# Transformer block on eight cores: the scalar engine's one-element copy after each softmax exponential is left out

## The chip, the cores and the metric

The program runs on all eight cores of one Trainium2 chip. Each core takes one of the eight sequences of the batch (4096 tokens of width 1024) and does the whole block on it; nothing passes between cores. The metric is the device time of the slowest core, in microseconds (us).

## What is computed

The reference adds to x (8 x 4096 x 1024) a full softmax attention of 16 heads over 4096 tokens, and after that a two-layer local-attention network. The change lies in the first part alone:

```
x = x + attn(layernorm(x));  x = x + ffn(layernorm(x))
q = einsum('bnd,hde->bhne', query, Wq) * scale     # E = 64, H = 16, scale = 1/8
k = einsum('bmd,hde->bhme', query, Wk);  v = einsum('bmd,hde->bhme', query, Wv)
attn = softmax(einsum('bhne,bhme->bhnm', q, k), axis=-1)
out = einsum('bhnm,bhme->bnhe', attn, v)
```

Then come two layers with a shifted token, a window of 512, xpos rotary tables, and a gated network of width 2730.

## The kernel before, in words

The instruction streams of the engines are written out by hand in program order. `op` (whose line 150 is the line of nearly every instruction in the profile) puts one instruction into an engine's list, with waits on semaphores ahead of it and increments behind it. For DVE and ACT, `op` adds two things on its own: a wait until every earlier instruction of the same engine has raised that engine's semaphore (`V` or `S`), and an increment by one when the instruction is done. `val('S')` is the count that the semaphore S will have after everything put into ACT's list so far. `sfence` puts a copy of one float (`fsc`, 1x1) into ACT's list and returns the count after it; `vfence` does the same on DVE.

Stage A (the first 5440 us or so) is the full attention. The 16 heads are taken in 4 groups of four (`grp`). A group first makes K (transposed, `KTg`) and V (`Vg`, 64 columns and one column of ones for each head) for all 4096 keys. Then, for each of 8 blocks of 512 queries (`qb`), it makes Q (`Qg`), runs for each of two head pairs (`p`) the inner loop over 32 chunks of 128 keys (`mc`), and multiplies the result by the output weights (`Wpg`). So the inner loop is run 4 x 8 x 2 = 64 times, with 32 chunks each.

One chunk of the inner loop is:

- S: two matmuls, one for each head of the pair, on two halves of the array (64 rows each), scores of 128 keys by 512 queries, into PSUM `pb1` for even and `pb3` for odd chunks. The first waits until the exponential of chunk mc-2 has read that PSUM tile.
- exp: one ACTIVATE on ACT, 128x1024, from `pb1` or `pb3` into `Pa` (even) or `Pb` (odd). It waits for S of its chunk and, through `op`, for every ACT instruction before it.
- the fence: a COPY of `fsc` on ACT. Its count is stored as `sexp[mc]`.
- AV: two matmuls (128 keys, 65 rows of output, 512 queries) from `Pa` or `Pb` that add to `pb5` and `pb6`. They wait for `sexp`.

TensorE's list holds S of chunk mc ahead of AV of chunk mc-1: S0, S1, AV0, S2, AV1, S3 and so on to AV31. Two waits tie the engines together: AV of chunk j waits for `sexp[j]`, and S of chunk j+2, which stands behind that AV, waits for the same count. In the text below a "pitch" is the time from the start of one exponential to the start of the next.

After the 32 chunks DVE takes the reciprocal of each head's sum (`drow`), TensorE spreads it, DVE scales into `Ost`, and the next pair's S may begin. In the profile all PSUM tiles (`pb0` to `pb7`) have the name `pb`.

The second part works in the same manner with buffers named `L0...` and `L1...` for its two layers. Its exponentials (`L0Ph`) have no copy behind each one: there the score matmuls wait for an ACTIVATE itself.

Of the kernel before, what the change touches and what calls it, by code (L numbers as in the profile page):

```python
# [97 lines left out]
class MK:  # L98
# [265 lines left out]
    def _stage_a(self):  # L364
# [127 lines left out]
        for grp in range(ngrp):  # L492
# [71 lines left out]
            for qb in range(NQB):  # L564
# [12 lines left out]
                for p in range(2):  # L577
                    sexp = {}
                    tavm = {}
                    p0exp = self.val('S')  # L580
                    for mc in range(33):
                        if mc < 32:
                            Sp = pb1 if mc % 2 == 0 else pb3
                            Pj = Pa if mc % 2 == 0 else Pb
                            wS = [('S', sexp[mc - 2])] if mc >= 2 else [('S', p0exp)]
                            self.op('T', 'matmul', Sp[:, 0:512],
                                    KT[p][0:64, mc * 128:(mc + 1) * 128],
                                    Qg[0:64, p * 512:(p + 1) * 512],
                                    start=True, stop=True, tile_position=(0, 0),
                                    wait=wS)  # L590
                            self.op('T', 'matmul', Sp[:, 512:1024],
                                    KT[p][64:128, mc * 128:(mc + 1) * 128],
                                    Qg[64:128, p * 512:(p + 1) * 512],
                                    start=True, stop=True, tile_position=(64, 0),
                                    inc=('T', 1))
                            ts = self.val('T')
                            we = [('T', ts)]
                            if mc - 2 in tavm:
                                we.append(('T', tavm[mc - 2]))
                            self.op('S', 'activation', Pj[:, :], Sp[:, :], AF.Exp,  # L600
                                    scale=0.125, wait=we)
                            sexp[mc] = self.sfence()
                        if mc >= 1:
                            j = mc - 1
                            Pj = Pa if j % 2 == 0 else Pb
                            self.wait('T', 'S', sexp[j])
                            self.op('T', 'matmul', pOa[0:65, :],
                                    Vg4[:, j, 2 * p, :], Pj[:, 0:512],
                                    start=(j == 0), stop=(j == 31))
                            self.op('T', 'matmul', pOb[0:65, :],  # L610
                                    Vg4[:, j, 2 * p + 1, :], Pj[:, 512:1024],
                                    start=(j == 0), stop=(j == 31),
                                    inc=('T', 1))
                            tavm[j] = self.val('T')
                    tav = self.val('T')
                    for hh, pO in ((0, pOa), (1, pOb)):
                        self.op('V', 'reciprocal', drow[0:1, :], pO[64:65, :],
                                wait=[('T', tav)] if hh == 0 else None, inc=('V', 1))
                        vr1 = self.vfence()
                        self.op('T', 'matmul', pm[0:64, 0:512], self.ones1b[0:1, 0:64],  # L620
                                drow[0:1, :], start=True, stop=True,
                                wait=[('V', vr1)], inc=('T', 1))
                        tb1 = self.val('T')
                        self.op('V', 'tensor_copy', dn[:, :], pm[0:64, 0:512], wait=[('T', tb1)])
                        self.op('V', 'tensor_tensor',
                                Ost[hh * 64:(hh + 1) * 64, p * 512:(p + 1) * 512],
                                pO[0:64, :], dn[:, :], op=ALU.mult, inc=('V', 1))
                    self.wait('T', 'V', self.vfence())
# [820 lines left out]
```

How the kernel before makes its waits and increments, by code:

```python
        def fn(e):  # L147
            for sm, v in wait:
                e.wait_ge(semh[sm], v)
            instr = getattr(e, meth)(*a, **kw)
            for sm, k in incv:
                instr.then_inc(semh[sm], k)
# [2 lines left out]
    def wait(self, eng, sem, v):  # L155
        semh = self.semh
        self.emit(eng, lambda e: e.wait_ge(semh[sem], v))
# [12 lines left out]
        def fn(e):  # L170
            for sm, v in toks:
                e.wait_ge(semh[sm], v)
```

## Time and profile before

| | us |
|---|---|
| median of two timed runs | 12493.09 (12472.9 and 12513.29) |
| the profiled execution, its time | 12375.73 |
| its span, first to last instruction of the slowest core | 12374.1 |
| ACT busy | 3587.4 (29% of the span) |
| TensorE matmuls busy | 6101.7 (49%) |
| DVE busy | 4237.4 (34%) |

The profile is of one execution, of its slowest core (core 0) where nothing else is said. Busy times are sums over the span, and the span holds stages with different limits, so a share says little by itself. PE is TensorE, PEld its weight loads. The granted clock is given in parts of full speed: 1.00 is 2.4 GHz, 0.50 is 1.2 GHz. In a timeline the columns are start (us from the span's start), duration (us), engine, line, operation, output<-input, shapes and count; neighbouring instructions of one kind are merged into one row with their count, and brackets hold the idle time of the engine before it and what ended it.

### The profile page before, as it was taken

How to read it: one execution, taken by the hardware profiler on the slowest of the kernel's cores; microseconds unless marked ns; L12 is line 12 of the kernel's file. 1: busy time of each engine (PE TensorE's matmuls, PEld its weight loads, DVE VectorE, ACT ScalarE, POOL GpSimd, SP SyncE). 2: the span in 40 equal slices, each digit the busy share in tenths (PEclk: the TensorE clock that was granted, in tenths of full speed). 3: DMA queues.
4: the chain of work that ended last, by engine and by line, in shares of the span. 5: the costliest groups of instructions: out<-in, count | busy, mean ns of one | idle time of the engine just before them, and what ended most of it. 6: DMA issues, size and time to landing. Idle time of an engine off the chain costs nothing.

```text
span 12374.1 us, 129139 instructions; the slowest of 8 cores (12332.9 to 12374.1 us)
## 1 busy us (share of the span) xinstructions
PE 6101.7 (49%) x36694; PEld 3084.5 (25%) x36694; DVE 4237.4 (34%) x8932; ACT 3587.4 (29%) x6788; POOL 270.1 (2%) x406
## 2 busy tenths in 40 slices
PE   2555555546555545533333333777733333346766
PEld 1111111112111211111111112665611111135665
DVE  5111221112111222235555553333345445523333
ACT  0555355544555245521111110111101111101111
POOL 0000000000000000000000000000000000000000
PEclk9788787778887777765555555888855555568888
DMA  3000001010000110120000003000010010041110
GB/s 116 14 14 14 21 12 17 14 18 14 14 14 14 35 40 28 35 62 17 17 23 29 17 18 75 22 28 28 19 44 17 17 34 17 18 86 42 33 41 28
DMA packets 237209, 361.42 MB, mean 29 GB/s; under 512 B 27664, under 2 KB 122512, under 8 KB 234468
## 3 DMA queue, kind: packets, MB, share of 16 engines
q0 software_dynamic: 51968, 101.01, 4.9%
q1 hardware_dynamic: 120036, 168.23, 4.3%
q10 hardware_dynamic: 64512, 83.91, 1.9%
q8 instruction: 315, 5.16, 0.2%
q14 instruction: 378, 3.10, 0.1%
HBM read 269.23 MB, written 134.35 MB: 33 GB/s over the span
## 4 chain that ended last, share of the span: by engine, by line
PE 33%; DVE 25%; ACT 22%; issue 9%; DMA 8%; DVEq 1%; ACTq 1%; POOL 0%; SPq 0%; POOLq 0%
PE pb L150 33%; ACT Pa L150 8%; ACT Pb L150 8%; DVE drow L150 3%; ACT fsc L150 3%; DVE fsc L150 2%; DVE L1drl L150 2%; DVE L0drl L150 2%; DMA yacc<-ysb 2%; DVE L0tmp L150 1%; ACT L0Ph L150 1%; DVE pb L150 1%; ACT L1Ph L150 1%; DVEq L149 1%; DMA L1dw<-w 1%
## 5 line engine op out<-in xcount | busy, mean ns | idle before, releaser
L150 ACT ACTIVATE Pa<-pb 128x1024 bf16<-128x1024 f32 x1024 | 1047.7, 1023 | 2558.2 <-PE pb L150 2473.1
L150 DVE RECIPROCAL drow<-pb 1x512 bf16<-1x512 f32 x128 | 429.0, 3352 | 3032.6 <-PE pb L150 3026.0
L150 ACT ACTIVATE Pb<-pb 128x1024 bf16<-128x1024 f32 x1024 | 1047.7, 1023 | 115.6 <-PE pb L150 22.4
L150 PE MATMUL pb<-Pa,Vg 128*65 128x512 bf16 x2048 | 655.5, 403 | 514.6 <-ACT fsc L150 508.5
L150 PE MATMUL pb<-Qg,KTg 64*128 64x512 bf16 x4096 | 842.3, 413 | 113.3 <-DVE fsc L150 113.3
L150 PE MATMUL pb<-Pb,Vg 128*65 128x512 bf16 x2048 | 653.6, 402 | 467.4 <-ACT fsc L150 465.0
L150 PE MATMUL pb<-L0dh,L0dw 128*128 128x256 bf16 x5632 | 703.1, 281 | 170.9 <-DVE fsc L150 170.9
L150 PE MATMUL pb<-L1dh,L1dw 128*128 128x256 bf16 x5632 | 702.3, 281 | 170.9 <-DVE fsc L150 170.9
L150 PEld LDWEIGHTS pb<-L0dh,L0dw 128*128 128x128 bf16 x5632 | 565.4, 101 | 261.1 <-issue 181.5
L150 PEld LDWEIGHTS pb<-L1dh,L1dw 128*128 128x128 bf16 x5632 | 565.4, 101 | 260.2 <-issue 181.5
L150 ACT COPY fsc<-fsc 1x1 f32<-1x1 f32 x2904 | 552.4, 190 | 255.3 <-ACT L1dgel L150 1.1
L150 DVE COPY fsc<-fsc 1x1 f32<-1x1 f32 x3161 | 448.2, 142 | 334.5 <-DVE pb L150 2.5
L150 PEld LDWEIGHTS pb<-Qg,KTg 64*128 64x128 bf16 x4096 | 202.1, 93 | 1017.5 <-issue 1017.1
L150 PE MATMUL pb<-Ost,Wpg 128*128 128x512 bf16 x512 | 259.1, 609 | 348.3 <-DVE fsc L150 348.3
L150 ACT ACTIVATE L1Ph<-pb,L1rk 128x512 bf16<-128x512 f32 (+1 forms) x480 | 253.0, 527 | 591.8 <-DVE fsc L150 563.5
L150 ACT ACTIVATE L0Ph<-pb,L0rk 128x512 bf16<-128x512 f32 (+1 forms) x480 | 253.0, 527 | 589.9 <-DVE fsc L150 522.8
L150 DVE TENSOR_TENSOR pb<-pb,M_sb 128x128 f32<-128x128 f32 x960 | 287.9, 300 | 340.0 <-PE pb L150 280.4
L150 PE MATMUL pb<-drow,ones1b 1*64 1x512 bf16 x128 | 76.9, 601 | 603.2 <-DVE fsc L150 603.2
L150 PE MATMUL pb<-L1du,L1dw 128*128 128x256 bf16 (+1 forms) x2816 | 364.9, 272 | 18.2 <-DVE fsc L150 18.0
L150 PE MATMUL pb<-L0du,L0dw 128*128 128x256 bf16 (+1 forms) x2816 | 365.0, 272 | 17.2 <-DVE fsc L150 17.2
L150 PEld LDWEIGHTS pb<-Pa,Vg 128*65 128x65 bf16 x2048 | 149.0, 112 | 823.4 <-issue 823.4
L150 PEld LDWEIGHTS pb<-Pb,Vg 128*65 128x65 bf16 x2048 | 148.5, 111 | 772.5 <-issue 772.5
(263 smaller groups left out, 7176.4 us busy)
## 6 DMA issues: line engine op xcount, KB each, us to landing
yacc<-ysb POOLq DMA_DIRECT2D x192, 256.0 KB, 4.1
xspan<-xT SPq DMA_DIRECT2D x16, 2048.0 KB, 10.2
yac<-yacc SPq DMA_DIRECT2D x64, 256.0 KB, 3.5
xsp<-xT SPq DMA_DIRECT2D x64, 256.0 KB, 3.9
R<-x1f ACTq DMA_DIRECT2D x64, 256.0 KB, 3.7
RA<-L0za ACTq DMA_DIRECT2D x64, 256.0 KB, 2.9
RZ<-L0dzot ACTq DMA_DIRECT2D x128, 128.0 KB, 1.7
RA<-L1za ACTq DMA_DIRECT2D x64, 256.0 KB, 3.0
```

Source lines behind the costliest of these rows:

```text
L149: e.wait_ge(semh[sm], v)
L150: instr = getattr(e, meth)(*a, **kw)
```

## The change

One expression in the inner loop of `_stage_a`: the count that is stored for chunk mc is that of the ACTIVATE itself, and the COPY behind it is no longer put into ACT's list.

```diff
                             self.op('S', 'activation', Pj[:, :], Sp[:, :], AF.Exp,
                                     scale=0.125, wait=we)
-                            sexp[mc] = self.sfence()
+                            sexp[mc] = self.val('S')
```

ACT's list from the first inner loop on, before (`fsc` is the copy; `pb1` and `pb3` are the two score tiles):

```order
3 L150 COPY fsc<-fsc 1x1 [waits S] x2
4 L150 ACTIVATE Pa<-pb1 128x1024 [waits T,S]
5 L150 COPY fsc<-fsc 1x1 [waits S]
6 L150 ACTIVATE Pb<-pb3 128x1024 [waits T,S]
7 L150 COPY fsc<-fsc 1x1 [waits S]
8 L150 ACTIVATE Pa<-pb1 128x1024 [waits T,S]
9 L150 COPY fsc<-fsc 1x1 [waits S]
```

ACT's list at the same place with the change:

```order
3 L150 COPY fsc<-fsc 1x1 [waits S] x2
4 L150 ACTIVATE Pa<-pb1 128x1024 [waits T,S]
5 L150 ACTIVATE Pb<-pb3 128x1024 [waits T,S]
6 L150 ACTIVATE Pa<-pb1 128x1024 [waits T,S]
7 L150 ACTIVATE Pb<-pb3 128x1024 [waits T,S]
8 L150 ACTIVATE Pa<-pb1 128x1024 [waits T,S]
```

One COPY goes for each exponential; each ACTIVATE keeps its wait for ACT's own count, which is now that of the ACTIVATE before it. TensorE's list is the same in both kernels, with the same waits. Here it is from the first chunk of the first loop on (`pb5` and `pb6` take the output of the two heads); `waits S` there is the count that now comes from the ACTIVATE:

```order
933 L150 MATMUL pb3<-Qg,KTg0 128x512 [waits S]
934 L150 MATMUL pb3<-Qg,KTg0 128x512
935 L150 MATMUL pb5<-Pa,Vg 65x512 [waits S]
936 L150 MATMUL pb6<-Pa,Vg 65x512
937 L150 MATMUL pb1<-Qg,KTg0 128x512 [waits S]
938 L150 MATMUL pb1<-Qg,KTg0 128x512
939 L150 MATMUL pb5<-Pb,Vg 65x512 [waits S]
940 L150 MATMUL pb6<-Pb,Vg 65x512
```

Nothing moved on TensorE, DVE, GpSimd or SyncE.

## Rows read from the trace of the kernel before

**Rows 1.** The cores: span and mean granted clock of the slowest

```profile
core 0: 12374.1 us, clock 0.729
```

**Rows 2.** The chain that ended last, by engine and by line

```profile
PE 33%; DVE 25%; ACT 22%; issue 9%; DMA 8%; DVEq 1%; ACTq 1%; POOL 0%; SPq 0%; POOLq 0%
PE pb L150 33%; ACT Pa L150 8%; ACT Pb L150 8%; DVE drow L150 3%; ACT fsc L150 3%; DVE fsc L150 2%; DVE L1drl L150 2%; DVE L0drl L150 2%; DMA yacc<-ysb 2%; DVE L0tmp L150 1%; ACT L0Ph L150 1%; DVE pb L150 1%; ACT L1Ph L150 1%; DVEq L149 1%; DMA L1dw<-w 1%
```

**Rows 3.** The page's costliest groups: busy us, mean ns | idle before, releaser

```profile
L150 ACT ACTIVATE Pa<-pb 128x1024 bf16<-128x1024 f32 x1024 | 1047.7, 1023 | 2558.2 <-PE pb L150 2473.1
...
L150 ACT ACTIVATE Pb<-pb 128x1024 bf16<-128x1024 f32 x1024 | 1047.7, 1023 | 115.6 <-PE pb L150 22.4
...
L150 ACT COPY fsc<-fsc 1x1 f32<-1x1 f32 x2904 | 552.4, 190 | 255.3 <-ACT L1dgel L150 1.1
```

**Rows 4.** Timeline, middle of an inner loop, 769 to 774 us

```profile
770.18 0.19 ACT L150 COPY fsc<-fsc 1x1 f32<-1x1 f32 x1
770.46 1.02 ACT L150 ACTIVATE Pa<-pb 128x1024 bf16<-128x1024 f32 x1
...
770.51 0.59 PE L150 MATMUL pb<-Pb,Vg 128*65 128x512 bf16 x2 [0.48 <-ACT fsc L150]
...
771.04 0.39 PE L150 MATMUL pb<-Qg,KTg 64*128 64x512 bf16 x2
771.57 0.19 ACT L150 COPY fsc<-fsc 1x1 f32<-1x1 f32 x1
771.85 1.02 ACT L150 ACTIVATE Pb<-pb 128x1024 bf16<-128x1024 f32 x1
```

**Rows 5.** Windows of 5 us between and inside inner loops: PEclk before the DMA share

```profile
950.00:955.00 5.00, 0.60 (x1) 0.12 (x1) 3.87 (x4) 0.00 (x0) 0.00 (x0) 0.50 0.00 0
...
965.00:970.00 5.00, 3.22 (x14) 0.85 (x14) 0.00 (x0) 4.36 (x8) 0.00 (x0) 1.00 0.00 0
```

**Rows 6.** Timeline, start of the inner loop at 957 us, and its end

```profile
957.55 1.02 ACT L150 ACTIVATE Pa<-pb 128x1024 bf16<-128x1024 f32 x1 [14.69 <-PE pb L150]
...
959.00 1.03 PE L150 MATMUL pb<-Pa,Vg 128*65 128x512 bf16 x2 [1.17 <-ACT fsc L150]
959.96 0.61 PE L150 MATMUL pb<-Qg,KTg 64*128 64x512 bf16 x2
...
960.50 1.06 PE L150 MATMUL pb<-Pb,Vg 128*65 128x512 bf16 x2
960.78 1.02 ACT L150 ACTIVATE Pa<-pb 128x1024 bf16<-128x1024 f32 x1 [0.54 <-PE pb L150]
...
963.91 1.02 ACT L150 ACTIVATE Pa<-pb 128x1024 bf16<-128x1024 f32 x1 [0.29 <-PE pb L150]
...
1001.68 1.02 ACT L150 ACTIVATE Pb<-pb 128x1024 bf16<-128x1024 f32 x1
...
1003.13 0.59 PE L150 MATMUL pb<-Pb,Vg 128*65 128x512 bf16 x2 [0.80 <-ACT fsc L150]
```

**Rows 7.** Timeline, window attention of layer 0, 6427 to 6430 us

```profile
6427.40 0.69 ACT L150 ACTIVATE L0Ph<-pb,L0rk 128x512 bf16<-128x512 f32 x1
...
6428.23 0.50 PE L150 MATMUL pb<-L0qf,L0kf 64*128 64x384 bf16 x2 [0.95 <-ACT L0Ph L150]
...
6428.56 1.47 ACT L150 ACTIVATE L0Ph<-pb,L0rk 128x512 bf16<-128x512 f32 x2 [0.47 <-DVE fsc L150]
```

**Rows 8.** Timeline, gated network of layer 0, 8620 to 8628 us, clock 1.00

```profile
8620.12 1.91 PE L150 MATMUL pb<-L0dh,L0dw 128*128 128x256 bf16 x16
...
8622.19 0.47 ACT L150 ACTIVATE L0dgel<-pb,L0b1t 128x256 f32<-128x256 f32 x1 [1.87 <-PE pb L150]
```

**Rows 9.** Timeline, first inner loop, 336 us, in a stretch of granted clock 0.81

```profile
336.20 0.69 PE L150 MATMUL pb<-Pa,Vg 128*65 128x512 bf16 x2 [0.33 <-ACT fsc L150]
...
336.83 0.44 PE L150 MATMUL pb<-Qg,KTg 64*128 64x512 bf16 x2
```

**Rows 10.** Window 2790 to 2850 us, core 2, making K and V

```profile
2790.00:2850.00 60.00, 55.13 (x372) 36.59 (x377) 31.70 (x97) 0.55 (x1) 0.00 (x0) 1.00 0.00 1
```

## The prediction

> **What bounds the kernel now.** I read the cores first, to see whose time counts: core 0 ends last, its span of 12374.1 us is the time to shorten [rows 1]. Then the chain that ended last. It has no single owner, but exponentials of the full attention (`Pa`, `Pb`) hold 16% of it and the one-element copy `fsc` on ACT another 3% [rows 2]. That is the copy that the change takes out, so it stands on the path somewhere. The groups say how much there is: 2 x 1024 exponentials of 1023 ns, and 2904 copies of 190 ns, of which 2048 go [rows 3]; the 64 inner loops have 32 chunks each, and 64 x 32 = 2048.
>
> Where the copy costs its time only the timeline shows. In the middle of a loop the exponential of 770.46 us ends at 771.48, the copy starts at 771.57, ends at 771.76, and the next exponential starts at 771.85 [rows 4]. So ACT works without a break: pitch 1.02 + 0.09 + 0.19 + 0.09 = 1.39 us, and the two starts lie 1.39 apart. TensorE waits for ACT: its AV pair starts 0.14 after the copy's end (770.37 to 770.51), with the copy as releaser. In this stretch ACT is the bound and everything else has slack.
>
> That holds for most pitches, not for all. Between loops TensorE is nearly idle and its granted clock is 0.50; inside it is 1.00 [rows 5]. The loop that begins at 957.55 starts at the low level: the AV pair takes 1.03 us in place of 0.59, the exponential of 960.78 is released by TensorE and not by ACT, and the fifth exponential (963.91) comes 6.36 us after the first, against 5.56 for four pitches of 1.39 [rows 6]. From there to the last one (1001.68) are 27 pitches in 37.77 us, 1.40 each. This loop takes 44.13 us from its first to its last exponential; in the timeline the other 63 look alike, with 3 to 5 long pitches at their start.
>
> **The change, part by part.** Removed: the copy (0.19) and one of the two gaps (0.09), 0.28 us for each exponential. Nothing is added and nothing is moved on another engine; TensorE's and DVE's instructions keep their order. What must be worked out is which limit comes next.
>
> ACT's own limit becomes 1.02 + 0.09 = 1.11 us. That two ACTIVATEs in a row have the same gap is seen in the second part: one of 128x512 takes 0.69, two take 1.47 together, so the gap is 0.09 [rows 7].
>
> The other limit is a round trip. The exponential of chunk j+2 needs S of chunk j+2, which stands behind AV of chunk j, which needs the exponential of chunk j. One trip covers two pitches. Its pieces:
> - the exponential, 1.023;
> - its end to the start of AV, without the copy. The nearest row is a score matmul that waits for an ACTIVATE directly: 6427.40 + 0.69 = 6428.09, start 6428.23, so 0.14 [rows 7]. It is the same 0.14 as behind the copy, so no extra price for leaving the fence;
> - start of AV to start of S, 770.51 to 771.04, 0.53, and S itself, 0.39 [rows 4];
> - end of S to start of exp. In the loop at low clock: 959.96 + 0.61 = 960.57, start 960.78, 0.21 [rows 6]. In the gated network at clock 1.00: 8620.12 + 1.91 = 8622.03, start 8622.19, 0.16 [rows 8].
>
> With 0.21 the trip is 1.023 + 0.14 + 0.53 + 0.39 + 0.21 = 2.293, or 1.147 a pitch; with 0.16 it is 1.122. With the copy it was 2.573, or 1.287, hidden below 1.39. So the cover of the round trip is gone: it is just above ACT's 1.11, and what is late next is S. I take 0.21, since that row is the same pair of instructions at the same place. A pitch in the fast stretch then gains 1.393 - 1.147 = 0.246. The bounds are 0.28 (ACT alone sets it) and, from the clock (below), 0.173.
>
> At the low clock TensorE itself is near its own limit: AV to S 0.96, S to AV 0.54, 1.50 a pitch [rows 6]. The second and third exponentials come 0.28 earlier (957.55 + 1.11; and 960.50, the trip from the first being 0.28 shorter). The fourth and fifth follow at 1.50 to 1.54, so the fifth comes at about 963.58 in place of 963.91: 0.33 gained, where 4 x 0.28 would be 1.12. That the clock rises at the same moment is assumed; TensorE is as busy there as before.
>
> At the end of the loop the last AV waits for the last exponential: 1001.68 + 1.02 = 1002.70, start 1003.13 [rows 6]. It gains the 0.28 whole, since DVE's reciprocal stands right behind it.
>
> Sum for a loop: 0.33 + 27 x 0.246 + 0.28 = 7.25 us. Times 64: 464 us, call it 465. All of it is on the path, since in the loop DVE, SyncE and GpSimd have nothing that others wait for; what follows (reciprocals, projection, the write of `yacc` by DMA) is released by the loop's end and only shifts. The loads of the next group's weights stand behind those writes in GpSimd's queue and shift with them, so they hide no more and no less. The second part of the program is untouched.
>
> Against its own time the profiled execution would go from 12375.7 to about 11911. The two timed runs lie 0.8 to 1.1% above it (median 12493.1), and I have no row that says why; I subtract the same 465 from the median: 12028 us. The level stays an unknown of some 117 us.
>
> **The rivals.**
>
> A. ACT alone sets the pitch, because S reaches exp in 0.16 or less and two trips interleave. For it: the 0.16 of rows 8 and a difference of only 0.034 between the two limits. Against it: the loop's own 0.21. Per loop 0.33 + 27 x 0.28 + 0.28 = 8.17, times 64 = 523: 11970.
>
> B. The clock goes down to the middle level under the denser work. TensorE's S and AV take 0.98 us of each pitch: 70% of 1.39 before, 86% of 1.147 after. In its first loop core 0 was granted 0.81, with AV to S 0.63 and S 0.44 [rows 9]: the trip is 1.023 + 0.14 + 1.07 + 0.21 = 2.44, 1.22 a pitch, gain 0.173. Before, that was hidden below 1.39, so the loop did not show it. Per loop 0.33 + 27 x 0.173 + 0.28 = 5.28, times 64 = 338: 12155. Against it: with TensorE busy for 55.13 of 60 us in making K and V, more than the 86%, core 2 was granted 1.00 [rows 10].
> The Trainium skill, "TensorE: Matmul & The Clock Gate", Part 1 (the clock gate), says that a peak-current limiter takes a die to 13/16 of the clock once three of its cores run dense matmuls. That speaks for B in every loop, as all cores do the same thing at nearly the same time. Rows 10 do not bear it out: the other cores of that die were in the same stage in that window. By that rule the sum would be that of B.
>
> C. The time goes up: TensorE does not leave its low clock in the loops, or leaves it late. The place is the fourth and fifth pitch of each loop, where it now rises. Then the pitch is TensorE's 1.50 against 1.39: 27 x 0.107 = 2.89 lost a loop, less 0.61 gained at both ends, 2.28 x 64 = 146 us, 12639. It decides the sign once fewer than 7 of the 27 later pitches are at full clock (0.246 f + 0.61 = 0.107 (27 - f)). Against it: denser work was granted 1.00, and I see no row where more work lowered it to 0.50.
>
> D. The copy was not what AV waited for, and AV still starts 0.42 after the exponential. Then ACT is free but the trip stays at 2.573: pitch 1.287, gain 27 x 0.106 = 2.86 + 0.3 a loop, some 200 us, 12290. Against it: the direct wait of rows 7.
>
> **How the numbers follow.** My forecast 0.74, A 0.12, B 0.09, C 0.02, D 0.03. The forecast's own doubt is small in the mechanism (between 1.12 and 1.16 a pitch, 40 us or so) and larger in the level of the runs (117 us). The range reaches down to A measured at the level of the profiled execution (12376 - 523 = 11853, of which I leave the last bit out) and up to B from the median (12155): 11870 to 12155. A measurement of this kernel can tell about 2% from no change, that is 250 us. The forecast, A and B are beyond that on the fast side; C and D are within it. I give a small part of C more than 2%, as its price would double if the clock fell elsewhere too: faster 0.95, same 0.04, slower 0.01.
>
> **What would show it right or wrong.** ACT's copies fall from 2904 to 856, about 390 us less busy. In the timeline of a loop's middle, exp starts lie 1.14 to 1.15 apart, ACT idles about 0.03 beyond its gap before each, with TensorE as the releaser, and AV starts 0.14 after the exponential's end. The releaser of AV is now the exponential. A loop takes about 37.1 us from first to last exponential in place of 44.13. Pitches of 1.11 mean A, of 1.22 beside a clock of 0.81 mean B, of 1.50 beside 0.50 mean C, of 1.29 mean D. The first five exponentials still take about 6 us. If the loops shorten as said and the time does not fall by about 465, the loss lies between the loops or in the second part, and the whole argument that nothing there is touched is wrong.

## The result, and the profile after

The changed kernel takes 11994.7 us (median of 11 runs, 11900.9 to 12059.8) against 12436.6 for the kernel before (10 runs): a ratio of 0.9631, with a 95% interval of 0.9588 to 0.9674, or 442 us less by the medians. The forecast was 465 us less and 12028 us.

In most executions of every kernel here, before and after, the cores of one die or of both are granted a clock of 0.81 in some stretches and end later than the others of the same execution (by up to 369 us before and 266 after), so a median compares mixtures, and where I want the effect of an edit alone I compare cores whose mean clock shows that they were left alone ("undisturbed cores"). Before, these end at 12333 to 12352 us (die 1 of the first profile, clock 0.731 to 0.733). After, in one timed run, at 11861 to 11877 (die 1, clock 0.724 to 0.726): 474 us less from middle to middle. The other executions agree: the median of all cores with a mean clock of 0.730 or more is 12352 us before, that of all with 0.724 or more after is 11877.

The page of the changed kernel: span, busy shares and the chain (what was [rows 2]), and the groups that answer to [rows 3].

```profile
span 11983.8 us, 124907 instructions; the slowest of 8 cores (11907.6 to 11983.8 us)
...
PE 6169.8 (51%) x36558; PEld 3139.7 (26%) x36694; DVE 4237.6 (35%) x8932; ACT 3197.5 (27%) x4740; POOL 270.0 (2%) x406
...
PE pb L150 34%; ACT Pa L150 8%; ACT Pb L150 8%; DVE drow L150 4%; DVE fsc L150 2%; DVE L1drl L150 2%; DVE L0drl L150 2%; DMA yacc<-ysb 2%; DVE L0tmp L150 1%; ACT L0Ph L150 1%; DVE pb L150 1%; ACT L1Ph L150 1%; DVEq L149 1%; DVE ysb L150 1%; DMA L1dw<-w 1%
...
L150 ACT ACTIVATE Pa<-pb 128x1024 bf16<-128x1024 f32 x1024 | 1047.6, 1023 | 2604.2 <-PE pb L150 2498.2
...
L150 ACT ACTIVATE Pb<-pb 128x1024 bf16<-128x1024 f32 x1024 | 1047.6, 1023 | 163.4 <-ACT Pa L150 80.4
...
L150 PE MATMUL pb<-Pa,Vg 128*65 128x512 bf16 x2048 | 650.8, 401 | 271.5 <-ACT Pa L150 271.3
```

From the groups of the same trace, the copies that are left:

```profile
L150 ACT COPY fsc<-fsc 1x1 f32<-1x1 f32 x856 | 162.8, 190 | 76.7 <-ACT L1dgel L150 1.1 <-ACT L0dgelb L150 1.1 <-ACT L1Ph L150 0.7
```

ACT's copies fall from 2904 to 856 and ACT's busy time from 3587.4 to 3197.5 us, 390 less. `ACT fsc`, 3% of the chain before, is no longer in it. The exponentials take the same 1023 ns. AV is now released by the exponential itself.

The timeline of the changed kernel in the middle of a loop (core 2), at the place that answers to [rows 4]:

```profile
1637.91 1.02 ACT L150 ACTIVATE Pa<-pb 128x1024 bf16<-128x1024 f32 x1
...
1639.08 0.59 PE L150 MATMUL pb<-Pa,Vg 128*65 128x512 bf16 x2 [0.20 <-ACT Pa L150]
1639.08 1.02 ACT L150 ACTIVATE Pb<-pb 128x1024 bf16<-128x1024 f32 x1 [0.15 <-ACT Pa L150]
1639.60 0.39 PE L150 MATMUL pb<-Qg,KTg 64*128 64x512 bf16 x2
1640.20 1.02 ACT L150 ACTIVATE Pa<-pb 128x1024 bf16<-128x1024 f32 x1
...
1640.78 0.39 PE L150 MATMUL pb<-Qg,KTg 64*128 64x512 bf16 x2
1641.37 0.59 PE L150 MATMUL pb<-Pa,Vg 128*65 128x512 bf16 x2 [0.20 <-ACT Pa L150]
1641.38 1.02 ACT L150 ACTIVATE Pb<-pb 128x1024 bf16<-128x1024 f32 x1 [0.15 <-ACT Pa L150]
```

Read it as two trips side by side. The `Pa` exponentials start at 1637.91 and 1640.20, the `Pb` ones at 1639.08 and 1641.38: each trip takes 2.29 to 2.30 us. From `Pa` to `Pb` it is 1.17 to 1.18 us, from `Pb` to `Pa` 1.12. In the `Pa` trip S ends at 1639.60 + 0.39 = 1639.99 and the exponential starts 0.21 later. In the `Pb` trip S is done at 1641.17 and the exponential starts at 1641.38, 0.21 again. The mean pitch is 1.146 us; the forecast said 1.147. An alternation was not forecast: here the `Pa` exponential starts at ACT's limit (1.11 to 1.12) behind the `Pb` one, and the `Pb` one takes what is left of the trip. Over all loops of this core the first 8 pitches of each left out, half of the pitches are near 1.12 and half near 1.18, apart from 2% longer ones.

The brackets need care. The profile names `ACT Pa`, not TensorE, as what ended the 0.15 us before each `Pb` exponential, since by its events `Pa` ended last (1641.22, S at 1641.17). But 0.15 is more than ACT's own gap of 0.09, and the start lies 0.21 behind the end of S, as in the `Pa` trip. That TensorE sets this pitch is therefore not read from the bracket; the run with S ahead of AV (below) shows it.

The start of the same loop answers to [rows 6]:

```profile
1632.31 1.02 ACT L150 ACTIVATE Pa<-pb 128x1024 bf16<-128x1024 f32 x1 [14.10 <-PE pb L150]
1633.42 1.02 ACT L150 ACTIVATE Pb<-pb 128x1024 bf16<-128x1024 f32 x1
...
1635.26 1.02 ACT L150 ACTIVATE Pa<-pb 128x1024 bf16<-128x1024 f32 x1 [0.81 <-PE pb L150]
...
1636.79 1.02 ACT L150 ACTIVATE Pb<-pb 128x1024 bf16<-128x1024 f32 x1 [0.51 <-PE pb L150]
```

With 1637.91 from the rows above, the pitches are 1.11, 1.84, 1.53 and 1.12: at the low clock TensorE still sets 1.5 a pitch, as before, and the fourth is already at full clock. Over all 64 loops the time from first to last exponential adds up to 2359 us, 36.9 a loop, against 2823 us, 44.1, before. That is 464 less; the 0.28 at each loop's end would bring 18 more.

Where does the span lose part of this? The first and last instruction of three ACT tiles divide it: the exponentials of stage A, and the GELUs of the gated network in the two layers. Columns after the name: count, duration ns min/median/max, first and last start in us. Before (core 0):

```profile
L150 ACT ACTIVATE Pa<-pb x1024: 1023/1023/1024, 308.9 to 5419.2; 128x1024 bf16<-128x1024 f32 x171
...
L150 ACT ACTIVATE L0dgel<-pb,L0b1t x176: 473/473/474, 7652.6 to 8962.3; 128x256 f32<-128x256 f32 x176
...
L150 ACT ACTIVATE L1dgel<-pb,L1b1t x176: 473/473/475, 10997.1 to 12346.7; 128x256 f32<-128x256 f32 x176
```

After (core 2):

```profile
L150 ACT ACTIVATE Pa<-pb x1024: 1023/1023/1024, 305.3 to 4947.9; 128x1024 bf16<-128x1024 f32 x171
...
L150 ACT ACTIVATE L0dgel<-pb,L0b1t x176: 473/473/474, 7185.1 to 8539.8; 128x256 f32<-128x256 f32 x176
...
L150 ACT ACTIVATE L1dgel<-pb,L1b1t x176: 473/473/475, 10557.4 to 11955.7; 128x256 f32<-128x256 f32 x176
```

The loops with all that lies between them take 4642.6 us instead of 5110.3, 468 less. Of 464 + 18 = 482 some 14 are given back between the loops. From the last exponential of a block's first pair to the first of its second pair it takes 15.28 us after and 15.65 before, so there the end's gain arrives. From one block to the next it takes 50.1 us after and 49.7 before: the Q matmuls there last 562 ns on average after and 522 before, so some of that work meets the low clock. The gated network takes 1354.7 us instead of 1309.7 in the first layer and 1398.3 instead of 1349.6 in the second: 94 us more, with not one instruction changed there. (Of the 390 us between the two profiles that leaves 16, less time in the windows of layer 1 for the most part.) The windows over those stages show why. Columns: busy us (instructions) of PE, PEld, DVE, ACT, POOL, then the granted clock, the DMA share and GB/s. Before, then after:

```profile
7653.00:8963.00 1310.00, 964.72 (x8423) 832.74 (x8421) 417.29 (x1270) 232.30 (x702) 0.00 (x0) 0.86 0.07 24
10998.00:12347.00 1349.00, 963.88 (x8412) 832.49 (x8413) 468.29 (x1390) 231.66 (x699) 0.00 (x0) 0.85 0.11 35
```

```profile
7186.00:8540.00 1354.00, 1012.53 (x8411) 856.40 (x8412) 417.28 (x1270) 231.57 (x699) 0.00 (x0) 0.82 0.07 24
10558.00:11956.00 1398.00, 1014.58 (x8411) 856.92 (x8412) 468.35 (x1390) 231.78 (x700) 0.00 (x0) 0.81 0.10 33
```

The same matmuls are busy for 48 to 51 us more at a lower mean clock; DVE and ACT are the same. That is the 94 us. Not every core of this profile lost them: on core 7 the two stages take 1306.6 and 1348.2 us, and its loss lies in stage A (4683.7 us). Whether the lower clock belongs to the change was the open question for the experiments.

### The profile page after: what moved, and what is told of

Its sections match the earlier page's. It is cut to its first block, busy times and chain, and to the rows that moved or that the text cites. A ratio compares the mean times of both kernels' runs of the same rounds, so it can differ in the third digit from the quotient of the medians.

```text
span 11983.8 us, 124907 instructions; the slowest of 8 cores (11907.6 to 11983.8 us)
## 1 busy us (share of the span) xinstructions
PE 6169.8 (51%) x36558; PEld 3139.7 (26%) x36694; DVE 4237.6 (35%) x8932; ACT 3197.5 (27%) x4740; POOL 270.0 (2%) x406
## 4 chain that ended last, share of the span: by engine, by line
PE 34%; DVE 26%; ACT 20%; issue 9%; DMA 9%; DVEq 1%; ACTq 1%; SPq 0%; POOL 0%; POOLq 0%
PE pb L150 34%; ACT Pa L150 8%; ACT Pb L150 8%; DVE drow L150 4%; DVE fsc L150 2%; DVE L1drl L150 2%; DVE L0drl L150 2%; DMA yacc<-ysb 2%; DVE L0tmp L150 1%; ACT L0Ph L150 1%; DVE pb L150 1%; ACT L1Ph L150 1%; DVEq L149 1%; DVE ysb L150 1%; DMA L1dw<-w 1%
## 5 line engine op out<-in xcount | busy, mean ns | idle before, releaser
L150 ACT ACTIVATE Pa<-pb 128x1024 bf16<-128x1024 f32 x1024 | 1047.6, 1023 | 2604.2 <-PE pb L150 2498.2
L150 ACT ACTIVATE Pb<-pb 128x1024 bf16<-128x1024 f32 x1024 | 1047.6, 1023 | 163.4 <-ACT Pa L150 80.4
L150 PE MATMUL pb<-L1dh,L1dw 128*128 128x256 bf16 x5632 | 737.3, 289 | 170.9 <-DVE fsc L150 170.9
L150 PE MATMUL pb<-L0dh,L0dw 128*128 128x256 bf16 x5632 | 735.9, 289 | 170.9 <-DVE fsc L150 170.9
L150 PEld LDWEIGHTS pb<-L1dh,L1dw 128*128 128x128 bf16 x5632 | 581.5, 104 | 277.9 <-issue 181.8
L150 PEld LDWEIGHTS pb<-L0dh,L0dw 128*128 128x128 bf16 x5632 | 581.3, 104 | 276.8 <-issue 181.7
L150 PE MATMUL pb<-L1du,L1dw 128*128 128x256 bf16 (+1 forms) x2816 | 383.9, 282 | 17.3 <-DVE fsc L150 17.3
L150 PE MATMUL pb<-L0du,L0dw 128*128 128x256 bf16 (+1 forms) x2816 | 383.1, 281 | 17.8 <-DVE fsc L150 17.7
L150 PEld LDWEIGHTS pb<-L1du,L1dw 128*128 128x128 bf16 (+1 forms) x2816 | 280.8, 101 | 67.2 <-issue 27.0
L150 PEld LDWEIGHTS pb<-L0du,L0dw 128*128 128x128 bf16 (+1 forms) x2816 | 280.4, 101 | 67.4 <-issue 27.4
```

What stands on the lines that cost most here:

```text
L150: instr = getattr(e, meth)(*a, **kw)
```

## The experiments

All times of "before" beside an experiment come from the same chip and the same hour.

**A copy behind every second exponential.**

```diff
-                            sexp[mc] = self.val('S')
+                            sexp[mc] = self.sfence() if mc % 2 else self.val('S')
```

> The copy is left out behind even chunks and kept behind odd ones, where AV waits for it. Theory (two limits: ACT's own work, and a round trip exp - AV - S - exp that covers two pitches): ACT needs 1.11 + 1.39 = 2.51 us for two chunks, the trip of the odd chunks is 2.573 us, the trip limits, so two pitches take 2.57, 1.29 each. In-loop gain against before 27 x 0.106 a loop; about 200 to 220 us in all, time near 12220. Rival 1 (ACT's list alone sets the pitch, half the copies go, so half the gain): two pitches take 2.51, 1.25 each, gain about 240 to 260 us. Rival 2 (the whole gain comes from each AV that need not wait for a copy, each chunk on its own): two pitches take 1.15 + 1.39 = 2.54.

Measured: 12276 us (3 runs), ratio to before 0.983 (0.976 to 0.990), so 212 us less by that ratio and 191 by the medians. Undisturbed cores of a timed run end at 12123 to 12137, 213 below before. The loops of core 6 add up to 2618 us, 205 less than before. The timeline (core 6):

```profile
659.65 1.02 ACT L150 ACTIVATE Pb<-pb 128x1024 bf16<-128x1024 f32 x1 [0.15 <-ACT Pa L150]
...
661.04 1.02 ACT L150 ACTIVATE Pa<-pb 128x1024 bf16<-128x1024 f32 x1
...
662.22 1.02 ACT L150 ACTIVATE Pb<-pb 128x1024 bf16<-128x1024 f32 x1 [0.15 <-ACT Pa L150]
```

From `Pb` to `Pb` it takes 2.57 us, in pitches of 1.39 and 1.18. ACT's own list would allow 2.51 and a sum of single pitches 2.54. The trip with one copy in it was worked out at 2.573: both rivals fall, the round trip stands.

**The copy stays, but AV does not wait for it.**

```diff
                             sexp[mc] = self.val('S')
+                            self.sfence()
```

> The copy stays in ACT's list, but AV waits for the exponential and not for the copy. Theory: at full clock ACT's own list limits at 1.39 us a pitch as before, and AV starts 0.14 us after the exponential's end (0.42 before). Gain only where TensorE limits: 0.33 us at the start and 0.28 at the end of each loop, 64 x 0.61 = 39 us, time within 0.5% of before (12400 to 12440 where before is 12437). Rival (the release of AV is what counted, ACT's occupancy is cheap): most of the 440 us stay gained, time near 12000, pitch 1.15 to 1.2.

Measured: 12469 us (8 runs) against 12467, ratio 1.0005 (0.9961 to 1.005). The undisturbed die of the profile ends at 12293 to 12330, some 31 us below before; the loops of core 0 add up to 2800 us against 2823. The timeline (core 5) shows what happened:

```profile
820.80 0.19 ACT L150 COPY fsc<-fsc 1x1 f32<-1x1 f32 x1
820.86 0.59 PE L150 MATMUL pb<-Pb,Vg 128*65 128x512 bf16 x2 [0.48 <-ACT Pb L150]
821.08 1.02 ACT L150 ACTIVATE Pa<-pb 128x1024 bf16<-128x1024 f32 x1
...
822.19 0.19 ACT L150 COPY fsc<-fsc 1x1 f32<-1x1 f32 x1
...
822.48 1.02 ACT L150 ACTIVATE Pb<-pb 128x1024 bf16<-128x1024 f32 x1
```

AV starts while the copy is still running, so it was released early as meant; the pitch is 1.39 or 1.40 all the same. What the copy cost at full clock was ACT's time, not TensorE's wait. Releasing AV early alone brings only what was worked out for the loops' ends and starts (39 us expected, 31 seen).

**S ahead of AV, with a third buffer.**

```diff
+        Pc = self.sbuf('Pc', [128, 1024], BF16, st=stA)
+        P3 = [Pa, Pb, Pc]
...
-                    for mc in range(33):
+                    for mc in range(34):
...
-                            Pj = Pa if mc % 2 == 0 else Pb
+                            Pj = P3[mc % 3]
...
-                            if mc - 2 in tavm:
-                                we.append(('T', tavm[mc - 2]))
+                            if mc - 3 in tavm:
+                                we.append(('T', tavm[mc - 3]))
...
-                        if mc >= 1:
-                            j = mc - 1
-                            Pj = Pa if j % 2 == 0 else Pb
+                        if mc >= 2:
+                            j = mc - 2
+                            Pj = P3[j % 3]
```

> On top of the change: a third buffer for the exponentials' result and S of chunk j+2 put ahead of AV of chunk j in TensorE's list, so the round trip is exp - S - exp only: 1.02 + 0.14 + 0.39 + 0.21 = 1.76 us for two pitches. Theory: ACT alone limits, every pitch of the fast stretch is 1.11 us, not alternating 1.11 and 1.18; 27 x 0.034 = 0.9 us a loop, 59 us in all; where the clock is 0.81 the trip of 1.22 goes too. Time 55 to 90 us below the changed kernel. Rival (the 1.15 is a delay inside ACT, not a wait for TensorE): pitches stay 1.11 and 1.18, time the same. At low clock TensorE's own work of 1.50 us a pitch stays.

Measured: 11925 us (6 runs), ratio to before 0.9593 (0.9558 to 0.9629). By the medians that is 69 us below the changed kernel, by the cores of die 0 of the profile (11773 to 11810) 77. The mean clock of these cores is 0.718 to 0.721, so I can't call all of them undisturbed by the clock alone. The interval of the ratio overlaps that of the change, so it is the timeline (core 7) that shows the effect:

```profile
831.15 1.02 ACT L150 ACTIVATE Pc<-pb 128x1024 bf16<-128x1024 f32 x1
831.21 0.39 PE L150 MATMUL pb<-Qg,KTg 64*128 64x512 bf16 x2 [0.17 <-ACT Pb L150]
831.53 0.62 PE L150 MATMUL pb<-Pb,Vg 128*65 128x512 bf16 x2
832.27 1.02 ACT L150 ACTIVATE Pa<-pb 128x1024 bf16<-128x1024 f32 x1
...
833.39 1.02 ACT L150 ACTIVATE Pb<-pb 128x1024 bf16<-128x1024 f32 x1
```

Every pitch is 1.12 and no bracket stands behind the exponentials: S ends 0.67 us before it is needed. The rest of the trip's 0.03 a pitch is gone, as is part of the low-clock start (35.3 us a loop from first to last exponential, on average, against 36.9). The limit now is ACT itself: 1.02 us of work and 0.09 of gap.

**The third buffer alone.** The same buffers and waits, TensorE's order as in the change.

> On top of the change: the third buffer for the exponentials' result alone, TensorE's order as in the change. Theory (S stands behind AV, so the exponential never waits for the buffer): pitches 1.12 and 1.18 as with two buffers, no difference. Rival (what e3 gained came from the third buffer and not from the order): pitches 1.12 throughout.

Measured: 12105 us (2 runs) against 12566; the undisturbed die ends at 11866 to 11893, as that of the change. The exponentials of core 4:

```profile
2330.86 1.02 ACT L150 ACTIVATE Pc<-pb 128x1024 bf16<-128x1024 f32 x1
2332.03 1.02 ACT L150 ACTIVATE Pa<-pb 128x1024 bf16<-128x1024 f32 x1 [0.15 <-ACT Pc L150]
2333.15 1.02 ACT L150 ACTIVATE Pb<-pb 128x1024 bf16<-128x1024 f32 x1
```

The next two start at 2334.33 and 2335.44: pitches of 1.17, 1.12, 1.18 and 1.11. The buffer does nothing, the order does it. The profile of this kernel also settled a second matter (below).

**The kernel before and the changed kernel once more.**

> The kernel before, unchanged, for a second profile. It tells whether the stretches of granted clock 0.81, 130 us a core on half the cores in the first profile of before and 460 to 790 us a core on all in that after the change, come with the denser work or with the execution. Theory (density): 0 to 200 us a core again, mean clock 0.729 to 0.733. Rival (chance of the execution): some 500 us a core here too, mean clock near 0.72.

> The changed kernel, unchanged, for a second profile and more times. Theory: the edit takes 7.5 us from each of 64 loops, 480 us, and the rest of the difference between executions is time at the granted clock 0.81, nearly all in the gated network. So a core that shows no 0.81 ends near 11865 (12345 to 12375 for such a core in the kernel before, less 480), and the pitches are 1.12 and 1.18 again. Rival (the second part is slower after the change for a reason of the change): cores without 0.81 end near 11960, as the first profile's 390 us would have it.

The kernel before ended at 12498.8 us in this execution. Its cores:

```profile
core 3: 12346.6 us, clock 0.727
...
core 7: 12497.3 us, clock 0.720
```

150 us lie between two cores of one execution of the same program. The theory that only the changed kernel has much 0.81 falls: the clock goes down in the kernel before too. Of the 151 us some 72 lie in the gated networks (1339.6 and 1386.5 us on core 7, 1305.1 and 1349.4 on core 3), the rest outside them; the inner loops have no part in it, they add up to 2825 and 2823 us. The changed kernel, again: median 12033 us against 12566, ratio 0.9627 (0.9539 to 0.9714), the same ratio as at first. In its profile all eight cores were disturbed (clock 0.705 to 0.714, 11927 to 12058 us). In another of its timed runs die 1 ended at 11873 to 11891 (clock 0.725 to 0.727), while die 0 took 11909 to 12000. The expected level was 11865, the rival's 11960: the rival falls, for an undisturbed core the second part is not slower after the change. Whether the change makes such stretches more frequent stays open: in the executions whose cores are on record, 33 before and 16 after, the median of a die's cores lies more than 20 us above the undisturbed level in 34 of 66 cases before and in 22 of 32 after, too few to tell.

The kernel with the third buffer alone gives both levels in one execution. Two cores, the gated network of the second layer, first a disturbed one (core 2), then one of the other die (core 4):

```profile
10611.00:12071.00 1460.00, 1080.45 (x8414) 889.94 (x8414) 468.14 (x1390) 232.34 (x700) 0.00 (x0) 0.77 0.10 32
```

```profile
10520.00:11866.00 1346.00, 962.33 (x8420) 831.33 (x8419) 468.31 (x1391) 232.15 (x700) 0.00 (x0) 0.85 0.11 35
```

The same 8400 matmuls of the same program take 118 us more at the lower mean clock, 114 of them in the stage's length. The first profile of the changed kernel had lost 45 and 49 us in its two stages of this kind, so such a clock is enough to explain them. What lies behind the mean shows in windows of 5 us in which TensorE is busy throughout: on core 2 it was granted 0.81 in 124 of them and 1.00 in 51, on each of the four cores of die 1 1.00 in 153 to 157 and 0.81 in at most one.

What 0.81 costs inside a loop can be read too. In the first profile of the changed kernel core 7 is at 0.81 at about 1040 us:

```profile
1020.00:1050.00 30.00, 25.81 (x100) 5.94 (x98) 0.00 (x0) 25.24 (x25) 0.00 (x0) 0.81 0.00 1
```

```profile
1036.98 1.02 ACT L150 ACTIVATE Pb<-pb 128x1024 bf16<-128x1024 f32 x1
1037.04 0.69 PE L150 MATMUL pb<-Pa,Vg 128*65 128x512 bf16 x2 [0.26 <-ACT Pa L150]
...
1038.31 1.02 ACT L150 ACTIVATE Pa<-pb 128x1024 bf16<-128x1024 f32 x1 [0.30 <-PE pb L150]
...
1039.42 1.02 ACT L150 ACTIVATE Pb<-pb 128x1024 bf16<-128x1024 f32 x1
```

A trip takes 2.44 us, pitches 1.33 and 1.11, mean 1.22: exactly rival B's price, in the stretches where it holds. In the kernel before such a stretch cost the loop nothing, as ACT's 1.39 hid it (2825 against 2823 us above). So the change does make the loops sensitive to this clock, by 0.07 us a pitch. Over the whole of stage A core 7 lost 41 us against core 2 of the same profile, 22 of them in the loops (2381 against 2359 us). S ahead of AV hides it again: there core 5, with 0.81 in several loops, has a sum of 2261 us against 2258 on core 1.

**Extra matmuls between the loops, to keep the clock up.**

```diff
                     tav = self.val('T')
+                    for _ in range(8):
+                        self.op('T', 'matmul', pb1[:, 0:512], Wp_g[0][:, 0:128],
+                                h[0][:, 0:512], start=True, stop=True)
...
                         tb1 = self.val('T')
+                        for _ in range(10 if hh == 0 else 6):
+                            self.op('T', 'matmul', pb1[:, 0:512], Wp_g[0][:, 0:128],
+                                    h[0][:, 0:512], start=True, stop=True)
```

> On top of the change: extra matmuls (128x128 by 512, results in a PSUM tile that nobody reads before it is overwritten) in TensorE's idle time between the inner loops: 8 after the last AV, 10 after the first head's spread, 6 after the second's. Leaves out nothing of the computation. Theory: the low clock at the start of a loop costs some 1.4 us a loop (loops that follow the K and V stage without a low-clock start took 35.5 us from first to last exponential, the mean is 36.9), so 64 x 1.35 = 86 us, and the spread matmuls at full clock give 2 x 0.2 x 64 = 25 more: 60 to 110 us below the changed kernel, pitches of 1.84 and 1.53 gone. Rival 1 (more busy TensorE brings more 0.81): the loops shorten but the second part or the loops run at 0.81 more often, the time stays within 30 us. Rival 2 (the extra matmuls are too few to lift the clock): nothing changes or the time rises by up to 50 us where they delay the spread.

Measured: the profile was of an undisturbed execution, 11803 to 11832 us on all cores, 51 below the change. The loops' sum of first-to-last times is 2333 us against 2359: 26 of the 51, a third of what was hoped for, since many loops still start low. The other 25 are the 128 spread matmuls, 396 ns each in place of 594, as expected. The five times have a median of 12072 us against 12496 before, not better than the change by itself. But in four of the five die 1 was at a mean clock of 0.72 to 0.73 and ended up to 313 us behind die 0, while die 0 ended at 11796 to 11827 in two of them. So the theory fits where the clock was left alone, and whether the extra work brings on the 0.81, as rival 1 has it, stays open: five runs can't tell that. I would not keep it.

**DVE's copies in stage A.** In the block loop `self.vfence()` becomes `self.val('V')`, six places.

> On top of the change: DVE's one-element copies in stage A's block loop (after the Q copy, the reciprocals, the scaling, the copy of the projection and, in the last group, the sums) are replaced by the count of the instruction before. Theory: these stand on the path, for TensorE waits for each: a copy of 0.14 and a gap of 0.10, 0.24 us each. In a block there are 2 for Q, 3 for each of two pairs, 8 for the projection, 16 in the last group (and more small work): 16 x 24 + 24 x 8 = 576 copies, 138 us if all are on the path; 110 to 140 us below the changed kernel. Rival (DVE's copy overlaps with the time the signal takes to reach TensorE): under 40 us.

Measured: DVE's copies fall from 3161 to 2585, the 576 that were counted. Median 11953 us (6 runs), ratio to before 0.9591 (0.9452 to 0.9731). In the profile all eight cores are undisturbed and end at 11744 to 11767: 114 below the change. That is 0.20 us for each copy, of the 0.24 that it takes with its gap, so most stood on the path.

**ACT's copy behind the GELUs.**

```diff
-                sgel = self.sfence()
+                sgel = self.val('S')
```

> On top of the change: the same edit on ACT's copy behind each GELU of the gated network, 704 copies in two layers, 197 us of ACT's time with their gaps. Theory: there TensorE works without a break and ACT idles before each GELU, so the copy is off the path: time within 20 us of the changed kernel apart from the execution's clock, pitch of the GELUs 2.62 us as before at full clock. Rival (a removed copy gives back its time wherever it stands, as in the inner loop): 150 to 200 us less.

Measured: 12050 us (2 runs). Die 1 of the profile ends at 11836 to 11899 (clock 0.723 to 0.726), against 11861 to 11891 for the change. The timeline (core 4):

```profile
8000.91 0.47 ACT L150 ACTIVATE L0dgelb<-pb,L0b1t 128x256 f32<-128x256 f32 x1 [2.15 <-PE pb L150]
8001.47 1.91 PE L150 MATMUL pb<-L0dh,L0dw 128*128 128x256 bf16 x16
...
8003.22 1.04 PE L150 MATMUL pb<-L0du,L0dw 128*128 128x256 bf16 x8
8003.53 0.47 ACT L150 ACTIVATE L0dgel<-pb,L0b1t 128x256 f32<-128x256 f32 x1 [2.15 <-PE pb L150]
```

GELUs start 2.62 us apart, as at clock 1.00 in the kernel before; ACT's idle time before each grew from 1.87 [rows 8] to 2.15 us, by the 0.28 that were freed. TensorE works without a gap here, and in the spans of these cores 704 copies with 197 us of ACT's time can't be told from the scatter. The stages by themselves are less scattered: the gated networks take 1298 to 1299 and 1338 to 1340 us on cores 4 and 5, against 1307 and 1348 on cores 6 and 7 of the change's first profile. So the copies were worth some 17 us of the 197. The theory stands and the rival falls.

**All one-element copies replaced by counts,** `vfence` and `sfence` only returning the count; with S ahead of AV, and without.

> The version with S ahead of AV and a third buffer, and in addition every one-element copy of the whole program (DVE's and ACT's) replaced by the count of the instruction before it. Theory: on the chain of the kernel before, DVE's copies hold 2% of the span, some 240 us at 0.14 each, with their gaps about 400 us; to that ACT's in the windows' attention, some 30. Sum about 430 below e3_s_ahead, 11925 - 430 = 11500. Rival: once the copies go, DVE's instructions run into each other's waits and the gain is only that of the stage A copies, 120 us: 11800.

> Every one-element copy of the program replaced by the count before it, with two buffers and TensorE's order of the change. Theory (the two edits of e8 add up, since one shortens the loops and the other mostly what lies between and behind them): cores without 0.81 end 70 us above those of e8 (11291 to 11313), at 11360 to 11390. Rival (S ahead needs the shorter waits between the loops, or the other way round): more than 110 or less than 30 us apart.

With S ahead: median 11476 us (4 runs), ratio to before 0.9179 (0.905 to 0.9308), 8.2% less, the fastest kernel here. Two cores of its die 1:

```profile
core 6: 11312.6 us, clock 0.727
core 7: 11291.2 us, clock 0.728
```

That is 490 us below the cores of die 0 in the profile of the run with S ahead alone, where 430 were expected: more of the copies in the second part were on the path than the 2% of the chain had it. Core 7 here against core 1 there: stage A is 135 us shorter, each gated network 48 (1257.9 and 1298.1 us), and the other 250 lie in the rest of the two layers. So in the gated network, too, something waited for the copies; ACT's were worth some 8 of the 48. Without S ahead: median 11653 against 12566 before (0.927). In its fastest run, 11405 us, the cores end at 11377 to 11404 (clock 0.727 to 0.730), 88 us above those of the version with S ahead. Expected were 70; the edits add up.

## Why the prediction was right, point by point

- **ACT is the bound in the loop, and the copy costs it 0.28 us:** right. With the copy kept and AV released early the pitch stays at 1.39.
- **No price for leaving the fence (0.14 from the end of ACTIVATE to AV):** right. 1638.93 to 1639.08 is 0.15 in the changed kernel.
- **The next limit is a round trip of 2.293 us for two pitches:** right. 2.29 to 2.30 measured, and 2.57 with one copy in it. The choice of 0.21 over 0.16 from the end of S to the exponential was the right one; A's even 1.11 did not come, and came at once when S was put ahead of AV. Over all loops the 27 later pitches took 1.401 us on average before and 1.155 after, 0.246 less, as forecast. One sign did not show as written: ACT does not wait a further 0.03 before each exponential with TensorE as the releaser, but 0.06 before every second one, with `ACT Pa` named.
- **At low clock TensorE sets about 1.50 to 1.54:** right, 1.84 for the second pitch and 1.53 for the third. The start of a loop was undervalued: over all loops its first four pitches fell from 6.28 to 5.68 us, 0.60 where 0.33 was forecast, since the fourth pitch is at full clock already in many loops, and three of the four loops behind the K and V stage start at full clock and take 35.5 us. So first to last fell by 464 us where 64 x 6.97 = 446 were forecast.
- **0.28 at the loop's end, all of it on the path:** in the sum, 482 us in the loops became 468 in stage A, and the rest went into the work between the blocks, part of it at low clock. "It only shifts" was not quite right.
- **The sum, 465 us:** 474 by undisturbed cores, 442 by the medians, inside the range either way.
- **The level of 117 us that no row explained:** the prediction took it for an offset common to both kernels; it is a scatter of each execution, and goes with the time at clock 0.81. The largest single losses are in the gated network, where TensorE is the bound (114 us in one stage above), but not all: 72 of 151 us in the second execution of the kernel before, and none on core 7 in the first profile of the change. That the median fell by 442 us and not by 474 is within this scatter; that the forecast was subtracted from a median of two runs and still came within 34 us of that of eleven is in part luck.
- **Rival B:** its price of 1.22 a pitch was exact, its reach was not: it holds in stretches, on some cores. The Trainium skill's rule in "TensorE: Matmul & The Clock Gate", Part 1 (13/16 of the clock once three cores of a die run dense matmuls), was set aside on one window. These runs take back half of that: the level of 0.81 it names is what die after die shows in dense work, and on die 0 and die 1 apart. But it is no fixed consequence here: with the third buffer all four cores of die 1 were granted 1.00 through the dense stretches of the gated network, while core 2 was granted 0.81 in most of them.
- **C and D:** the low clock in the loops did not last longer, and AV did wait for the copy and for nothing else.

## What to carry to other kernels

A one-element instruction that serves only as a fence costs what its engine is worth at that place: 0.28 us each on ACT where ACT sets the pace (2048 of them gone took 3.7% off the time here), about 0.20 on DVE where TensorE waits behind it, and some 0.02 behind the GELUs, where TensorE is the bound. When a cost is taken off the bounding engine, work out the round trip through the others before pricing the gain, with its pieces read from the same loop; here it stood 3% above the new limit, and one exchange in TensorE's order with a third buffer removed it. And where cores of one execution differ by more than the effect looked for, compare cores, or single stages, that were left at the same clock, not medians.

## What the runs showed of the hardware that was not expected

- The granted clock of 0.81 comes and goes by die and by execution in the same program: a core with it ended at 12497 us and one without much of its cost at 12347 in a single execution of the kernel before, and at 12099 and 11866 to 11893 in one with the third buffer.
- Two trips that share ACT settle in an uneven rhythm (1.12 and 1.18) and hold it for the whole loop, rather than an even 1.146.
- An increment raised by an ACTIVATE reached TensorE in 0.14 to 0.15 us, the same as one raised by the one-element COPY, for outputs of 128x1024.
